# Layer 0 of a four-layer attention kernel: the output product issued ahead of the second transposes

## What is computed

```
h = Wq_list[i] @ z[:, :, half i] + Wi_list[i] @ u[:, :, half i]     # q, k, v of all heads
score = einsum('bndi,bndj->bnij', q + r_w_bias, k) * 64 ** -0.5      # 256 x 256 per head
prob = softmax(score)
attn_vec = einsum('bnij,bndj->bndi', prob, v)
x = Wo @ attn_vec + bo + z
return (x - mean(x)) * rsqrt(var(x) + 1e-5)
```

## Time and profile before

| | us |
|---|---|
| median of 3 runs | 1385.88 (1384.08 to 1386.36) |
| the profiled execution | 1384.41 |
| its span, first to last instruction | 1382.6 |
| layer 0 in it | about 401 of the span, 64 units |

### The profile page before, as it was taken

One profiled execution on the slowest core, in us unless ns is written; L12 is line 12 of the kernel. 1 busy time (PEld: TensorE's weight loads), 2 busy tenths in 40 slices (PEclk: granted clock), 3 DMA queues, 4 the chain that ended last, 5 costly groups with the idle time before them and its releaser, 6 DMA issues.

```text
span 1382.6 us, 24470 instructions
## 1 busy us (share of the span) xinstructions
PE 1277.6 (92%) x8912; PEld 1008.2 (73%) x8912; DVE 828.4 (60%) x1900; ACT 740.8 (54%) x2040; POOL 540.8 (39%) x571
## 2 busy tenths in 40 slices
PE   6999999999988988999999999999998986787788
PEld 5777777777644556899999889999985654645555
DVE  4666666766547985666666776666673029638620
ACT  4665555555545884555554655455544147647631
POOL 3554444544339983331121413121202039439420
PEclk9999999999998999999999999999999998997989
DMA  6101011010010003020111111020001010000000
GB/s 254 49 26 51 26 37 40 26 51 26 5 64 0 2 1 131 18 69 32 47 32 47 33 45 58 20 69 14 12 1 61 0 61 1 1 16 1 1 8 23
DMA packets 15525, 50.44 MB, mean 36 GB/s; under 512 B 1840, under 2 KB 5296, under 8 KB 14384
## 3 DMA queue, kind: packets, MB, share of 16 engines
q1 hardware_dynamic: 15408, 48.87, 10.6%
HBM read 47.82 MB, written 1.05 MB: 35 GB/s over the span
## 4 chain that ended last, share of the span: by engine, by line
PE 81%; DVE 12%; ACT 3%; issue 2%; POOL 1%; DMA 0%; SPq 0%; DVEq 0%; POOLq 0%
PE pS L1648 12%; PE acc L315 6%; PE pT L1676 6%; PE acc L1728 6%; PE pC L378 5%; PE pT L365 5%; PE pS L348 4%; PE pS L1690 4%; PE acc L334 4%; PE pC L1713 4%; DVE stats L1299 3%; PE acc L921 3%; PE acc L390 3%; PE pT L1452 2%; PE heads_transposed L1136 2%
## 5 line engine op out<-in xcount | busy, mean ns | idle before, releaser
L1648 PE MATMUL pS<-split_sources,split_pair_weights 128*128 128x512 f32 x768 | 211.9, 411 | 5.8 <-issue 4.3
L665 POOL TENSOR_TENSOR probs<-probs,stats 128x512 f32<-128x512 f32 x128 | 130.6, 1042 | 182.4 <-DVE stats L543 182.4
L486 ACT ACTIVATE probs<-pS,stats 128x256 f32<-128x256 f32 x256 | 118.1, 473 | 136.2 <-DVE stats L538 136.2
L1648 PEld LDWEIGHTS pS<-split_sources,split_pair_weights 128*128 128x128 f32 x768 | 135.8, 190 | 30.7 <-issue 6.6
L1825 ACT ACTIVATE probsT<-pT 128x256 f32<-128x256 f32 x128 | 49.3, 385 | 197.0 <-PE pT L1701 197.0
L1728 PE MATMUL acc<-l_wo_parts,l_ctx_parts 128*128 128x256 f32 x768 | 121.9, 295 | 1.0 <-DVE l_ctx_parts L1897 1.0
L538 DVE TENSOR_REDUCE stats<-pS 128x2 f32<-128x512 f32 x128 | 82.4, 686 | 62.0 <-PE pS L348 61.9
L1676 PEld LDWEIGHTS pT<-l_wv_parts,split_sources 128*128 128x128 f32 x756 | 106.9, 188 | 14.2 <-issue 2.2
L1676 PE MATMUL pT<-l_wv_parts,split_sources 128*128 128x256 f32 x756 | 110.6, 281 | 2.1 <-issue 2.1
L1951 POOL TENSOR_TENSOR split_pair_weights<-weights_a,split_pair_weights 128x1024 fp32r<-128x1024 f32 x16 | 38.1, 2382 | 170.0 <-ACT split_pair_weights L1789 170.0
L315 PE MATMUL acc<-split_sources,split_pair_weights 128*128 128x512 f32 x372 | 101.9, 409 | 1.0 <-POOL split_pair_weights L652 0.7
(11 more groups left out here) (206 smaller groups left out, 2976.4 us busy)
## 6 DMA issues: line engine op xcount, KB each, us to landing
weights_a<-in_l_w SPq DMA_DIRECT2D x16, 768.5 KB, 4.3
weights_a<-in_l_w SPq DMA_DIRECT2D x16, 768.0 KB, 5.8
value_bias_rows<-in_l_bv SPq DMA_DIRECT2D x16, 256.0 KB, 4.4
weights_b<-in_l_wo SPq DMA_DIRECT2D x16, 256.0 KB, 2.7
w_fc<-in_l_w SPq DMA_DIRECT2D x4, 1024.0 KB, 6.0
bias_rows<-in_rows SPq DMA_DIRECT2D x1, 1536.0 KB, 13.4
x_residual<-in_x_dbl SPq DMA_DIRECT2D x2, 512.0 KB, 7.0
masked_scores<-in_ctx_dbl SPq DMA_DIRECT2D x2, 512.0 KB, 7.9
```

What stands on the lines that cost most here:

```text
L486: a = e.activation(self.E[:, n % 4, h, it, :], self.S[h][:, it, :], ACT.Exp, bias=self.st[:, 1, n % 4, h, it:it + 1], accum_out=self.st[:, ...
L665: e.tensor_tensor(self.E[:, n % 4, h, :, :], self.E[:, n % 4, h, :, :], self.st[:, 3, n % 4, h, :].unsqueeze(2).broadcast_to([P, 2, D]), A ...
L1648: mm = e.matmul(bank[:, :], self.w_qk[i % 2][kw][:, 1 - which, c, h * P:h * P + P], g.split[:, which, ks, c, half * HALF:half * HALF + HAL ...
```

## The change

The call of O moves from the end of the step to the place between Q and T1. Nothing else changes: the same instructions with the same waits.

```
             if n + 4 < self.N:
                 project_v(n + 4)
                 project_qk(n + 4)
+            if 0 <= n - 4 < self.N:
+                output(n - 4)
             if 0 <= n - 2 < self.N:
                 transposes(n - 2, 1)
             if 0 <= n - 3 < self.N:
                 context(n - 3)
-            if 0 <= n - 4 < self.N:
-                output(n - 4)
             for b in range(4):
                 if n == self.SUM_STEP[b]:
                     sum_transposes(b)
```

## The result

| | before | after |
|---|---|---|
| median, us | 1384.88 (1384.08 to 1386.36, 5 runs) | 1370.73 (1370.53 to 1375.67, 5 runs) |
| profiled execution / its span | 1384.41 / 1382.6 | 1375.67 / 1373.8 |
| first S / first F of the end / the distance | 21.97 / 400.49 / 378.52 | 22.50 / 389.05 / 366.55 |
| from there to the end | 982.13 | 984.80 |

The ratio of the means is 0.9909, with a 95% interval of 0.9889 to 0.9930: the kernel is faster by about 0.9%. (The medians differ by 1.0%: three of the five runs after took 1370.5 to 1370.7 us, two 1375.1 and 1375.7.) The forecast of 1373.0 (1370 to 1377) holds. Over all runs of the study, 19 of before and 9 of after, the means are 1384.90 and 1372.50, a difference of 12.4 us.

What follows compares the result with a forecast made beforehand. PE was taken to bound layer 0 without a gap, so only its own pitch counts. Ordinary steps 9.6, F or B steps 0.4 and last steps 2.2 sum to 12.2 us off the 1385.2 mean: 1373.0 us, range 1370 to 1377.

Steps and rivals of the forecast that it cites:

- The ordinary step: 48 layer 0 steps without F or B: O from 0.63 to 0.43 us, step 5.87 to 5.67, 9.6 us in all.
- The price of the direct switch: C followed straight by S, columns to rows: between 0.21 and 0.35 us, taken as 0.31.
- Step 3: Early step without O, where C is already followed by S: 0.35 us from last C pair to S, the upper bound.
- F and B steps: Eight steps ending in F or B: O falls, F's first transpose pays an exposed load; net 0.05 each, 0.4 us.
- The last steps: From step 60 on, O falls into PE's wait before T1: 2.8 us gained, 0.65 lost at the end, 2.2 net.
- Behind layer 0: Stages after layer 0 unchanged, gain carried to the end; half-speed clock stretches may shift it 1.5 us either way.
- The exposed loads: Rival: O's two fp32 loads are not hidden behind Q, O keeps 0.63 us; 1384.3 us; chance 0.04.
- The dear switch: Rival: columns to rows passes the whole-array state, 0.73 us instead of 0.31; 1393.2 us, slower; chance 0.03.
- the free one: Rival: the direct switch from C to S costs nothing extra, 4.8 us more gain; 1368.2 us; chance 0.05.
- The border waits: Rival: DVE's key part or fuller steps delay S at 14 group borders and steps 36 to 42; 1376; chance 0.06.
- the release "DVE l_keys_parts" ahead of S: Sign of being wrong: S released by DVE's key part every fourth step; 0.40 us of slack was expected there.
- The fuller steps: Steps 34 to 42, where DVE also has an add, statistics or normalisation: maxima may slip up to 0.8 us.

Runs made afterwards that it cites:

- the steps with 3, 4, 4 and 5 switches: Ordinary steps of the changed kernel, the kernel before, that with C ahead of T1, and that with O between C's halves: 5.67, 5.87, 5.82 and 6.02 us.
- the second: The changed kernel profiled and timed once more, with no edit: 1372.55 us, ratio 0.9911 to the kernel before.
- the kernel with the old end: Against the changed kernel, steps 66 and 67 back in the old order, C of unit 63 ahead of O of unit 62: 1370.85 us, one timed run.

## Why the prediction was right

- **What bounds.** Right. In the ordinary steps layer 0 is PE's alone, before and after: the distances in them are set by PE's own pitch. In the last steps DVE's copies and adds have their part, as the prediction said. DVE's idle of 1.10 us before the maxima fell to 0.48, the number that the prediction had.
- **The ordinary step.** O 0.43, C to S 0.31, step 5.67: all as written. The saving is 0.19 to 0.20 a step, so 48 steps bring some 9.3 us, and 9.6 was a little large: 0.63 - 0.43 in rounded numbers, where the distances were 0.628 and 0.430, and 5.867 to 5.673.
- **The price of the direct switch** was the open term, between 0.21 and 0.35. The value taken, by likeness to the two switches around O, was exact. Step 3 had bounded it from above before anything was run. That the array runs empty at a switch is not seen in any row; what the rows show is the price, and the steps with 3, 4, 4 and 5 switches show that it goes by their number.
- **F and B steps.** 6.04 us, 0.05 less than before: right, though these eight gave only 0.4 us. That C to F would cost a load was the reason for moving F later on.
- **The last steps.** Forecast 2.2, measured 2.3 (27.82 against 30.13). Of the parts, the gain up to the context products of unit 62 was put at 2.8 and came to 2.9, the loss behind them was put at 0.6 to 0.7 and came to 0.55, which the kernel with the old end confirms (0.54).
- **Sum.** 12.2 forecast for layer 0, 378.52 - 366.55 = 11.97 measured. The first F was expected near 388.3 and stood at 389.05, since the first S came 0.53 later than in the profile of before: what comes ahead of the first S differed between profiles of the same kernel as well (22.50 and 21.31), and the cause is open.
- **Behind layer 0.** The gain is carried to the end, less or more what the stretches at the lower clock do. I gave these 1.5 us either way. It was 2.7 against the gain in the first profile and 1.1 in the second. The runs near 1370.6 us have no profile; with a span of 1368.7 us, 366.5 for layer 0 and a first S between 21.3 and 22.5, 980 to 981 us must have followed, 1.3 to 2.5 in the gain's favour, and their mean granted clock is higher, 0.979 against 0.973. This is the one term that was too small. With it the median, 1370.73, came within 0.7 us of the range's lower end: that it stayed inside is in part luck. The mean of all nine runs, 1372.50, is the better test.
- **The rivals.** The exposed loads did not come: O's two loads hide behind Q and even behind the short transposes (0.21 to 0.22 between O's two records in either place). The prediction had set a rule of the Trainium skill beside this rival, "TensorE: Matmul & The Clock Gate", Part 3, that a load overlaps running matmuls only when the row group differs; the trace does not agree, for O's first load begins with Q's last record, at 202.92, on the same rows. The dear switch was refuted at 0.31, and so was the free one. The border waits show up by name only, without a time: the release "DVE l_keys_parts" ahead of S, 14 times in the list above, which the prediction had named as a sign of being wrong, came, and the steps are 5.67 us all the same. It was a bad sign, since it names the last semaphore and not a delay. The fuller steps did reach PE where O, F, B or C stood elsewhere: by DVE in step 42 of the kernels with B behind Q (6.50 us) and with O behind T1 (6.27), by ACT in steps 38 and 46 of the one with C ahead of T1 (6.56 and 6.34).

## What to carry to other kernels

Where an engine is busy without a gap, read the distances between starts at each place where the shape of the work changes, and count these places: here, at full clock and in fp32, each new division of PE's array cost 0.15 to 0.20 us, whichever product followed. Group what uses the array alike, and put the independent product either among its own kind or, where PE waits for a copy, into that wait. A bound for an adjacency that the steady loop doesn't have can often be read in its first or last rounds, where a stage is missing.

## What the runs showed of the hardware

- Three, four and five changes of the array's division in otherwise equal steps took 5.67, 5.82 to 5.87 and 6.02 us. A change from column halves to row halves costs the same 0.31 between starts (0.10 over the stream) as one from or to the whole array. The statement of the Trainium skill, "TensorEngine Tiling (Array Packing)", Key Properties, that changing the mode drains the engine agrees with all of them.
- A full-array fp32 load of 0.19 us hid behind matmuls of 0.21 us pitch that used the same rows. In the kernel with O behind T1 it began with the last of four transposes, and O's first record started 0.11 us behind that transpose, the transposes' own pitch.
- The time at the lower clock behind layer 0 varied between 61 and 75 us in ten profiles, and what followed layer 0 by 4 us with it; for one and the same kernel it was 68.3 and 75.1, and 1.6 us. A gain of 2 us in one run says nothing for that reason; the distance from the first S to the F of the end repeated to 0.02 us.
